# First mixture layer: twelve shared-expert chunks issued beside the first twelve expert tiles, and the ranks' results put in the logits' PSUM bank

## The chip, the cores and the metric

The kernel runs on one core of one Trainium2 chip. The metric is the time of one execution on the device in microseconds (us). The kernel before takes 1175.41 us, the median of three runs (1174.6 to 1175.93).

## The reference, cut to what matters

The program computes two transformer layers on x of 4 batches x 1024 tokens x 128 channels. The change touches only the feed-forward part of the first layer, a mixture of eight experts, two per token, with one shared expert that every token passes:

```python
logits = x_flat @ gate_w.T                      # 8 experts
scores = softmax(logits); in_topk = top 2       # w = scores * in_topk
gu = einsum('nh,eih->nei', x_flat, experts_gate_up); g, u = split(gu, 176)
out = einsum('nei,ehi->neh', silu(g) * u, experts_down) weighted by w
shared = silu(x_flat @ shared_gate_w.T) * (x_flat @ shared_up_w.T) @ shared_down_w.T   # width 352
out = out + sigmoid(x_flat @ shared_expert_gate_w.T) * shared
x = x + gb * out
```

## The kernel before, in words

The 4096 tokens are 32 tiles of 128 (NT = 32), 8 tiles to a batch (NB = 4 batches, TPB = 8). The mixture layer is one function, `layer_phase`, in which each engine has a queue written out by hand: first the engine's part of `route_parts`, then its part of `experts_parts`. Nothing but semaphores ties the queues together.

**Routing stage** (`route_parts`). For each batch b: VectorE computes statistics (L97 to L105) and the normalised rows h in two halves of four tiles (`rows`, L1297 to L1306); TensorE transposes each half into PSUM bank 0 (`transpose`, L1475), ScalarE copies it out to hT (L1411), TensorE makes the router's logits in bank 1 (`logits`, L1484); VectorE picks the top two (`experts_of`, L1312 to L1334); TensorE sums the ranks (`ranks`, L1490 to L1493) into bank 0, the transposes' bank; VectorE turns them into row numbers (`places`, L1340 to L1359), and GpSimd scatters the batch's rows to the buffer xg in memory by 16 indirect DMAs (L1232). Because `rank_ps` lies in bank 0, `transpose` of the next batch waits until the ranks of this one have been read (`ranked`).

**The shared expert** is cut into slabs of 512 tokens (8 of them) and its width of 352 into M = 3 chunks (128, 128, 96): 24 chunks n, `NU = 24`. A chunk is two products gate and up on TensorE (`up`, L1501, four matmul records of 512 columns), Silu on ScalarE (`shared`, L1430), the product on VectorE (`products`, L1368), and four matmuls of the down projection on TensorE (`down`, L1512, eight records). Three chunks accumulate one slab in bank 6 or 7 in turn; then ScalarE scales it out with four instructions (`shared_out`, L1438). The queues are: TensorE issues, for batch b, slab 2b, weights of expert 2b (`transpose_weights`, L1069 to L1076), transposes and logits of batch b+1, slab 2b+1, ranks of batch b+1, weights of expert 2b+1. So all 24 chunks are done before the first expert tile: the experts' TensorE part waits for `sh_out >= 8` at L1734 to L1742. The experts' weights and the chunks' gate/up results share banks 2 to 5 in turns; `pair_freed` says what a turn waits for.

**Tile stage** (`experts_parts`). 72 tiles of 128 gathered rows (NSLOT = 72). Tile n: SP loads 128 rows from xg (L1619); TensorE transposes them (`t_in`, L1734), ScalarE copies (L1641), VectorE copies the tile's expert weights (`lay_gate`, L1681), TensorE makes gate and up (`up`, L1742, six records), ScalarE Silu (L1652, L1653), VectorE the product (L1687 to L1690), TensorE down (L1759, four records), ScalarE scales (L1661), GpSimd scatters 128 rows to yk (L1632). The loops are skewed: TensorE's step n issues t_in(n+2), up(n+1), down(n-1). The first wave is tiles 0 to 39; their loads wait for the scatters of batches 0 to 2 and for VectorE's `tables`. GpSimd's queue holds all 64 row scatters ahead of the tiles' 72. VectorE also adds the finished shared expert to x, in eight instructions (L1698, L1703), one at each n = 8, 16, ... 64.

The second layer has the same two stages with other sizes; its work is as before.

Of the kernel before, what the change touches and what calls it, by code (L numbers as in the profile page):

```python
# [14 lines left out]
P = 128  # L15
# [975 lines left out]
NE = 8  # L991
# [13 lines left out]


# [98 lines left out]
def route_parts(nc, w, d, layer, ctx, bank):  # L1105
# [43 lines left out]
    rank_ps, total_ps = pT[:, 0:TPB * NE], pT[:, TPB * NE:TPB * NE + NE]  # L1149
# [11 lines left out]
    if layer == 0:  # L1161
# [5 lines left out]
        turn_of_chunk = lambda n: 2 + n + n // M  # L1167
        turn_of_weights = lambda e: 2 + (M + 1) * e + M
# [7 lines left out]
        def pair_freed(pe, turn, weights_out):  # L1176

            if turn < 2:
                return
            if turn < 4:  # L1180
                pe.wait_ge(weights_out, 1)
                return
            e, n = divmod(turn - 4, M + 1)
            if n == M:
                pe.wait_ge(weights_out, e + 2)
            else:
                pe.wait_ge(hid_done, M * e + n + 1)

        def weights_freed(pe, e, weights_out):
            pair_freed(pe, 0 if e == NE else turn_of_weights(e), weights_out)  # L1190
# [96 lines left out]

    def vector_part(dve):
# [73 lines left out]
        def products(s):  # L1362
            for n in range(M * s, M * s + M):
                cw = cols[n % M]
                dve.wait_ge(s_done, n + 1)

                after(dve, d_ps, n - 1)
                v.tensor_tensor(hid[n % 2][0:cw, :], sg[n % 2][0:cw, :], pg[0:cw, turn_of_chunk(n) % 2, 1, :], ALU.mult).then_inc(hid_done, 1)  # L1368

# [13 lines left out]
        for b in range(NB):  # L1383
            if layer == 0:
                for s in WEIGHTS_AT[b][0]:
                    products(s)
# [7 lines left out]
            if layer == 0:  # L1394
                for s in WEIGHTS_AT[b][1]:
                    products(s)
            if b + 1 < NB:
                places(b + 1)
                if b + 2 < NB:
                    rows(b + 2)  # L1400

    def scalar_part(act):
# [21 lines left out]
        def shared(s):  # L1424
            for n in range(M * s, M * s + M):
                cw = cols[n % M]
                act.wait_ge(g_ps, n + 1)

                after(act, hid_done, n - 1)
                nc.scalar.activation(sg[n % 2][0:cw, :], pg[0:cw, turn_of_chunk(n) % 2, 0, :], ACT.Silu).then_inc(s_done, 1)  # L1430
                if n % M == 1 and s > 0:
                    shared_out(s - 1)

        def shared_out(s):
            act.wait_ge(d_ps, M * (s + 1))
            for j in range(4):
                t = 4 * s + j
                ins = nc.scalar.activation(w.sh[:, t, :], pd[:, s % 2, j * C:(j + 1) * C], ACT.Copy, scale=w.shw[:, t:t + 1])  # L1438
            ins.then_inc(sh_out, 1)

# [12 lines left out]
        for b in range(NB):  # L1453
            for e in WEIGHTS_AT[b][0]:
                if layer == 0:
                    shared(e)
                copy_weights(act, e)
            if b + 1 < NB:
                batch(b + 1)
            for e in WEIGHTS_AT[b][1]:  # L1460
                if layer == 0:
                    shared(e)
                    if b + 1 < NB:
                        exponentials(b + 1)
                copy_weights(act, e)
        if layer == 0:
            shared_out(2 * NB - 1)

    def tensor_part(pe):
        def transpose(s):  # L1470
            pe.wait_ge(h_done, s + 1)
            after(pe, hT_done, s)
            after(pe, ranked, s // 2)
# [21 lines left out]

        def up(n):
            m, turn = n % M, turn_of_chunk(n)

            pair_freed(pe, turn, w_copied)
            for k in range(2):  # L1500
# [1210 lines left out]
```

## Time and profile before

| what | value |
|---|---|
| time of the runs, median of 3 | 1175.41 us (1174.6 to 1175.93) |
| span of the profiled execution | 1294.9 us |
| mean granted TensorE clock in it | 0.854 of full |
| ranks of batch 0 to first expert matmul, first layer (558.4 to 709.9) | 151.5 us |
| first expert matmul to the end of the tile stage (to 845.5) | 135.6 us |
| second layer's tile stage (1082 to 1262) | 180 us |

The profiled execution has no time of its own beside its span of 1294.9 us, so its own time is at least that; it is 119.5 us, 10.2%, above the median of the runs. In the profile, PE is the matmul side of TensorE, DVE is VectorE, ACT ScalarE, POOL GpSimd and SP the sync engine; ends of matmul records are modelled, and start times are what their spacing should be read from.

### The profile page before, as it was taken

To read this page: it belongs to the slowest core of one execution; us is meant where nothing else is said; L and a number is where in the kernel's file an instruction comes from. 1 tells how busy PE (TensorE), PEld (TensorE's weight loads), DVE (VectorE), ACT (ScalarE), POOL (GpSimd) and SP (SyncE) were. 2 spreads that over 40 slices of the span, in tenths; PEclk is the share of its full clock that TensorE was granted. 3 is DMA by queue.
4 is the path that set the end of the run, shared out by engine and by line. 5 is a ranking of instruction groups with operands and counts; after the bars stand their busy time and mean duration, and the time that the engine had idled before them with its cause. 6 is when DMAs were issued, how large, how long until landed. Compare 5 with 4: busy or idle time off the path is not lost. (4 is left out here: it accounts for less than half of the span.)

```text
span 1294.9 us, 26945 instructions
## 1 busy us (share of the span) xinstructions
PE 968.1 (75%) x9019; PEld 636.3 (49%) x9019; DVE 843.4 (65%) x2115; ACT 680.8 (53%) x1445; POOL 442.2 (34%) x510
## 2 busy tenths in 40 slices
PE   4656999999999999667576788718665427789990
PEld 2333333443343334344354677617543426679990
DVE  6897899999999996655431645556838555324444
ACT  3773678788788777324423555527022124436660
POOL 5626122332222122143234556510000733564440
PEclk9785799999999999867778989959687557989995
DMA  7235021111111000111110232276533311122216
GB/s 203 74 126 198 3 82 43 35 55 46 35 55 38 26 2 2 40 50 36 35 42 33 63 83 75 69 223 179 140 103 88 98 57 36 59 77 67 64 57 200
DMA packets 116285, 97.16 MB, mean 75 GB/s; under 512 B 15437, under 2 KB 102568, under 8 KB 116152
## 3 DMA queue, kind: packets, MB, share of 16 engines
q1 hardware_dynamic: 101912, 75.29, 20.4%
q0 software_dynamic: 8704, 17.97, 4.1%
q10 hardware_dynamic: 5536, 2.18, 0.6%
q8 instruction: 76, 1.25, 0.4%
q14 instruction: 57, 0.47, 0.1%
HBM read 60.18 MB, written 34.95 MB: 73 GB/s over the span
## 5 line engine op out<-in xcount | busy, mean ns | idle before, releaser
L568 DVE TENSOR_REDUCE part<-sps 128x2 f32<-128x1024 f32 (+2 forms) x307 | 327.6, 1115 | 27.0 <-PE sps L556 15.6
L911 ACT ACTIVATE prob<-tpa 128x1024 f32<-128x1024 f32 (+1 forms) x208 | 193.1, 928 | 45.1 <-PE tpa L857 43.3
L1632 POOL DMA_INDIRECT yk<-yo,place x144 | 146.6, 1018 | 158.1 <-ACT yo L1661 139.6
L743 POOL TENSOR_SCALAR_AFFINE_SELECT prob<-prob 128x512 f32<-128x512 f32 x128 | 80.5, 641 | 310.3 <-ACT prob L911 310.3
L1232 POOL DMA_INDIRECT xg<-h,slot x128 | 126.9, 991 | 152.1 <-DVE slot L1359 96.7
L877 PE MATMUL ops<-prob,vs 128*32 128x512 f32 (+3 forms) x1536 | 157.9, 498 | 0.1
L911 ACT ACTIVATE prob<-tpb 128x512 f32<-128x512 f32 (+1 forms) x224 | 127.2, 568 | 37.3 <-PE tpb L857 37.2
L549 PE MATMUL sps<-qk 48*128 48x512 bf16 (+2 forms) x734 | 132.9, 339 | 11.3 <-DVE part L568 7.6
L1687 DVE COPY place<-xt 128x1 uint32<-128x1 uint32 x144 | 22.1, 153 | 169.5 <-ACT esg L1655 92.5
L1748 PE MATMUL banks<-xT,y 128*128 128x128 f32 x864 | 113.8, 283 | 20.1 <-ACT y L1646 12.2
L1748 PEld LDWEIGHTS banks<-xT,y 128*128 128x128 f32 x864 | 106.5, 198 | 23.6 <-ACT xT L1641 19.3
L857 PE MATMUL tpa<-qk 50*128 50x512 bf16 (+3 forms) x512 | 85.6, 324 | 5.3 <-ACT prob L911 5.2
L857 PE MATMUL tpb<-qk 50*128 50x512 bf16 (+3 forms) x256 | 82.7, 343 | 5.2 <-DMA qk<-mrow 3.6
L1742 PE MATMUL banks<-xT,up_at 128*128 128x128 f32 (+1 forms) x432 | 68.3, 299 | 23.7 <-DVE up_at L1681 12.6
L1661 ACT ACTIVATE yo<-banks,xt 128x128 f32<-128x128 f32 x144 | 53.2, 369 | 45.8 <-PE banks L1759 35.8
L549 PEld LDWEIGHTS sps<-qk 48*128 48x128 bf16 x734 | 41.3, 94 | 71.9 <-DVE part L568 48.8
L1742 PEld LDWEIGHTS banks<-xT,up_at 128*128 128x128 f32 (+1 forms) x432 | 58.0, 202 | 31.2 <-ACT xT L1641 21.3
L556 PE MATMUL sps<-half 64*128 64x128 bf16 x976 | 66.5, 207 | 0.0
L857 PEld LDWEIGHTS tpa<-qk 50*128 50x128 bf16 x512 | 28.1, 94 | 69.3 <-ACT prob L911 61.2
L1759 PE MATMUL banks<-down,y 128*128 (+1 forms) x432 | 61.7, 281 | 0.2 <-issue 0.2
L556 PEld LDWEIGHTS sps<-half 64*128 64x128 bf16 x976 | 51.6, 97 | 20.8 <-issue 2.0
L1655 ACT ACTIVATE esg<-banks 128x384 f32<-128x384 f32 x72 | 35.5, 494 | 45.8 <-PE banks L1748 41.0
(347 smaller groups left out, 1864.8 us busy)
## 6 DMA issues: line engine op xcount, KB each, us to landing
xt<-xg SPq DMA_DIRECT2D x144, 65.0 KB
qk<-term SPq DMA_DIRECT2D x24, 256.0 KB, 2.6
qk<-qk SPq DMA_DIRECT2D x64, 96.0 KB
arena<-kpad SPq DMA_DIRECT2D x6, 1024.0 KB, 12.3
powers<-powr SPq DMA_DIRECT2D x8, 516.0 KB, 5.3
powr<-powers SPq DMA_DIRECT2D x4, 1032.0 KB, 9.3
qk<-qk SPq DMA_DIRECT2D x64, 64.0 KB
h<-yk SPq DMA_DIRECT2D x16, 256.0 KB, 4.9
```

The costliest lines, as they stand in the source:

```text
L549: ins = nc.tensor.matmul(out[:, s, at * wd:(at + 1) * wd], qk[lo:lo + KR, 0, x, i * P:(i + 1) * P], qk[lo:lo + KR, 1, x, c0:c0 + wd], star ...
L556: ins = nc.tensor.matmul(out[:, s, (at + 1) * wd - P + 64 * u:(at + 1) * wd], w.half[lo:lo + 64, 0, u, :], w.half[lo:lo + 64, 1, u, 64 * u ...
L568: return nc.vector.tensor_reduce(to, src, AX.X, ALU.max, negate=True)
L743: nc.gpsimd.affine_select(out=blk, in_=blk, pattern=[[0, HQ], [1, P]], compare_op=ALU.is_ge, fill=0.0, base=0, channel_multiplier=-1).then ...
L857: ins = nc.tensor.matmul(slot_of(t, m)[:, bank, col:col + n], qk[t % 4][lo:lo + KR + 2, 1, x, j * P:(j + 1) * P], qk[t % 4][lo:lo + KR + 2 ...
L877: ins = nc.tensor.matmul(ops[32 * h:32 * h + 32, o0:o0 + n], vs[t % 2][:, j, h, :], prob[:, PBUF[c] * HQ + u, col:col + n], start=c in OPE ...
L911: nc.scalar.activation(prob[:, at:at + len(units), 0:n], slot_of(t, m)[:, :, 0:n], ACT.Exp, scale=float(HD) ** -0.5).then_inc(exp_done, 1)
L1232: nc.gpsimd.indirect_dma_start(out=d.xg[layer], out_offset=bass.IndirectOffsetOnAxis(ap=w.slot[:, k, t:t + 1], axis=0), in_=w.h[k][:, t, : ...
L1632: nc.gpsimd.indirect_dma_start(out=d.yk, out_offset=bass.IndirectOffsetOnAxis(ap=place[:, u:u + 1], axis=0), in_=yo[u][:], in_offset=None) ...
L1742: ins = nc.tensor.matmul(pg[n % 2][0:cw, m * P:(m + 1) * P], up_at[n % WST][:, m * P:m * P + cw], xT[n % 4][:], start=True, stop=True)
L1748: ins = nc.tensor.matmul(out[:, m * P:(m + 1) * P], up_at[n % WST][:, (k * M + m) * P:(k * M + m + 1) * P], xT[n % 4][:], start=True, stop ...
L1759: ins = nc.tensor.matmul(pd[n % 2], hid[n % WST][0:cw, m, :], wt[0:cw, m, :], start=m == 0, stop=m == M - 1)
```

## The change

It has four parts. (1) In the first layer, only chunks 0 to 11 (slabs 0 to 3, `EARLY = 12`) stay in the routing stage, one slab per batch instead of two: chunk 3b ahead of batch b+1's transposes, chunks 3b+1 and 3b+2 and the last `down` behind its logits, the ranks behind them. Both weights of a batch go first. (2) Chunks 12 to 23 are issued in the tile stage, one in each of the steps n = 0 to 11, at the end of each engine's step (`late_tensor`, `late_scalar`, `late_vector`). They use one pair of banks (turn 1) and one accumulation bank, 6 (`bank_of_half`), so the first `down` of a late slab waits for the `shared_out` of the slab before it. (3) `rank_ps` and `total_ps` move to bank 1, with the logits; `transpose` no longer waits for `ranked`, and `logits` waits for it. The tile stage's transposes take one bank instead of two in the first layer, and t_in(n) waits for one copy more. (4) The eight additions of the shared expert to x come at n = 24, 28, ... 52 instead of n = 8, 16, ... 64.

```diff
+SUMS_AT = 24
-    WEIGHTS_AT = [([2 * b], [2 * b + 1]) for b in range(NB)]
+    WEIGHTS_AT = [([2 * b, 2 * b + 1], []) for b in range(NB)]
+    EARLY = M * NB
-    rank_ps, total_ps = pT[:, 0:TPB * NE], pT[:, TPB * NE:TPB * NE + NE]
+    rank_ps, total_ps = pl[:, P:P + TPB * NE], pl[:, P + TPB * NE:P + TPB * NE + NE]
+        bank_of_half = lambda s: s % 2 if s < NB else 0
+        TURNS = 2 + M
+        turn_of_weights = lambda e: TURNS * (e // 2) + e % 2
+        turn_of_chunk = lambda n: TURNS * (n // M) + 2 + n % M if n < EARLY else 1
...
 # VectorE, routing: products of chunk M*b ahead of tables/statistics/experts_of, the other two behind experts_of
+                shared_product(dve, M * b)
...
+                for n in range(M * b + 1, M * b + M):
+                    shared_product(dve, n)
...
 # ScalarE, routing
             for e in WEIGHTS_AT[b][0]:
                 copy_weights(act, e)
+                shared_silu(act, M * b)
             if b + 1 < NB:
                 batch(b + 1)
+                shared_silu(act, M * b + 1)
+                    exponentials(b + 1)
+                for n in range(M * b + 2, M * b + M):
+                    shared_silu(act, n)
+                shared_out(act, b)
...
+    def shared_down(pe, n):
+        m, s = n % M, n // M
+        pe.wait_ge(hid_done, n + 1)
+        if m == 0:
+            after(pe, sh_out, s if n >= EARLY else s - 1)
...
         def transpose(s):
-            after(pe, ranked, s // 2)
         def logits(s):
-            after(pe, lg_out, b)
+            after(pe, ranked, b)
...
 # TensorE, routing: both weights, shared_up(M*b), batch(b+1), then
+                for n in range(M * b + 1, M * b + M):
+                    shared_up(pe, n)
+                    shared_down(pe, n - 1)
+                shared_down(pe, M * b + M - 1)
+                if b + 1 < NB:
                     ranks(b + 1)
...
+    def late_tensor(pe, k):
+        if k <= NU - EARLY:
+            if k < NU - EARLY:
+                shared_up(pe, EARLY + k)
+            if k > 0:
+                shared_down(pe, EARLY + k - 1)
+    def late_scalar(act, k):
+        if k < NU - EARLY:
+            shared_silu(act, EARLY + k)
+        if k >= M + 1 and k % M == 1 and k <= NU - EARLY + 1:
+            shared_out(act, (EARLY + k) // M - 1)
+    def late_vector(dve, k):
+        if k < NU - EARLY:
+            shared_product(dve, EARLY + k)
...
 # experts_parts, first layer
-    pT, pd = [bank[:, 0, 0:P], bank[:, 6, 0:P]], ...
+    pT, pd = [bank[:, k, 0:P] for k in ((0, 0), (0, 6))[layer]], ...
-            after(pe, in_T, n - 1)
+            after(pe, in_T, n if layer == 0 else n - 1)
-                    pe.wait_ge(routed.sh_out, 2 * NB)
+                    pe.wait_ge(routed.hid_done, routed.early)
+                    pe.wait_ge(routed.sh_out, NB)
```

## Rows read from the trace of the kernel before

**Rows 1.** The page's first line

```profile
span 1294.9 us, 26945 instructions
```

**Rows 2.** Stretches of routing, then tile stage; columns PE, PEld, DVE, ACT, POOL, clock, DMA, GB/s

```profile
558.40:595.80 37.40, 27.50 (x95) 17.25 (x96) 16.34 (x77) 12.91 (x24) 16.31 (x16) 0.71 0.12 37
595.80:637.50 41.70, 26.40 (x111) 17.51 (x110) 16.82 (x77) 14.97 (x31) 15.37 (x16) 0.75 0.13 39
637.50:677.60 40.10, 26.99 (x113) 18.27 (x111) 18.38 (x80) 12.19 (x28) 15.64 (x16) 0.74 0.17 47
677.60:709.90 32.30, 20.64 (x102) 13.28 (x100) 7.28 (x20) 12.04 (x33) 15.37 (x16) 0.84 0.10 34
709.90:845.50 135.60, 107.89 (x790) 97.97 (x790) 70.56 (x315) 76.40 (x286) 75.46 (x71) 0.93 0.26 70
```

**Rows 3.** Waits of the routing stage: who for whom, us in total, times, longest

```profile
PE banks L1475 <- issue: 23.6, 3, 10.9
ACT sg L1430 <- remote: 9.0, 1, 9.0
```

**Rows 4.** Timelines of PE and ACT at batch 2's transposes: start, us, what, idle before

```profile
612.24 0.60 PE L1475 MATMUL banks<-ident,h 128*128 128x128 f32 x4
...
623.04 0.59 ACT L1411 COPY v<-banks 128x512 f32<-128x512 f32 x1 [6.28 <-remote]
```

**Rows 5.** Timelines of PE and POOL in the tile stage

```profile
714.82 0.83 PE L1742 MATMUL banks<-xT,up_at 128*128 128x128 f32 x6
...
716.04 0.83 PE L1742 MATMUL banks<-xT,up_at 128*128 128x128 f32 x6
...
845.35 0.96 POOL L1632 DMA_INDIRECT yk<-yo,place  x1 [0.30 <-issue]
```

**Rows 6.** The second layer's tile stage as one stretch

```profile
1082.00:1262.00 180.00, 161.89 (x1359) 158.60 (x1360) 67.78 (x237) 98.61 (x283) 90.77 (x93) 0.96 0.22 63
```

**Rows 7.** The stretch behind the late signal of rows 4

```profile
623.70:631.30 7.60, 7.58 (x24) 5.67 (x25) 3.03 (x31) 4.31 (x5) 0.00 (x0) 0.50 0.01 2
```

**Rows 8.** PE's timeline: two chunks that follow each other at full clock

```profile
632.27 1.88 PE L1501 MATMUL banks<-v,shgu 128*128 128x512 f32 x4
...
634.88 1.88 PE L1501 MATMUL banks<-v,shgu 128*96 128x512 f32 x4
```

**Rows 9.** DVE's timeline: the links of one batch's chain

```profile
549.74 0.69 DVE L1306 TENSOR_TENSOR h<-h,modr 128x512 f32<-128x512 f32 x1
...
552.75 0.17 DVE L105 SCALAR_TENSOR_TENSOR t<-t 128x8 f32<-128x8 f32 x1
...
554.86 0.23 DVE L1312 COPY lg<-banks 128x72 f32<-128x72 f32 x1 [1.94 <-PE banks L1484]
...
586.17 0.23 DVE L1312 COPY lg<-banks 128x72 f32<-128x72 f32 x1 [8.93 <-PE banks L1484]
...
589.68 0.19 DVE L1334 COPY run<-cum 128x8 bf16<-128x8 bf16 x1
...
598.29 0.22 DVE L1349 TENSOR_TENSOR row<-banks,first_row 128x64 f32<-128x64 f32 x1
...
604.77 1.28 DVE L1368 TENSOR_TENSOR hid<-sg,banks 128x512 f32<-128x512 f32 x2
```

**Rows 10.** ACT's timeline: table load, Silu of a chunk, a slab's four output instructions

```profile
679.82 1.28 ACT L1430 ACT_TABLE_LOAD   x1
681.11 0.60 ACT L1430 ACTIVATE sg<-banks 128x512 f32<-128x512 f32 x1
...
694.77 1.14 ACT L1438 ACTIVATE y<-banks,shw 128x128 f32<-128x128 f32 x4
```

**Rows 11.** Groups by line: the row scatters, and one half of the additions to x

```profile
L1232 POOL DMA_INDIRECT xg<-h,slot x64 | 62.7, 979 | 96.4 <-DVE slot L1359 78.1 <-issue 18.3
L1703 DVE TENSOR_TENSOR x<-x,y 128x1024 f32<-128x1024 f32 x4 | 4.8, 1211 | 0.0
```

**Rows 12.** POOL's timeline: the first of the row scatters

```profile
562.88 1.20 POOL L1232 DMA_INDIRECT xg<-h,slot  x1 [19.89 <-DVE slot L1359]
```

More of the change, by code:

```diff
@@ L1400, in vector_part, with shared_silu, shared_out @@
                     rows(b + 2)
+    def shared_silu(act, n):
+        cw = cols[n % M]
+        act.wait_ge(g_ps, n + 1)
+        after(act, hid_done, n - 1)
+        nc.scalar.activation(sg[n % 2][0:cw, :], pg[0:cw, turn_of_chunk(n) % 2, 0, :], ACT.Silu).then_inc(s_done, 1)
+    def shared_out(act, s):
+        act.wait_ge(d_ps, M * (s + 1))
+        for j in range(4):
+            t = 4 * s + j
+            ins = nc.scalar.activation(w.sh[:, t, :], pd[:, bank_of_half(s), j * C:(j + 1) * C], ACT.Copy, scale=w.shw[:, t:t + 1])
+        ins.then_inc(sh_out, 1)
     def scalar_part(act):
@@ L1422, in exponentials @@
             nc.scalar.activation(w.shw[:, s], lg[:, s, NE], ACT.Exp, scale=-1.0).then_inc(ex_done, 1)
[L1424 to L1439, printed above, removed]
         def batch(b):
@@ L1454, in scalar_part, with shared_up @@
             for e in WEIGHTS_AT[b][0]:
-                if layer == 0:
-                    shared(e)
                 copy_weights(act, e)
+            if layer == 0:
+                shared_silu(act, M * b)
             if b + 1 < NB:
                 batch(b + 1)
+            if layer == 0:
+                shared_silu(act, M * b + 1)
[4 more added lines that the diff above has]
+                shared_out(act, b)
             for e in WEIGHTS_AT[b][1]:
[L1461 to L1464, printed above, removed]
                 copy_weights(act, e)
-        if layer == 0:
-            shared_out(2 * NB - 1)
+    def shared_up(pe, n):
+        m, turn = n % M, turn_of_chunk(n)
+        if n < EARLY:
+            pair_freed(pe, turn, w_copied)
+        else:
+            pe.wait_ge(hid_done, n)
+        for k in range(2):
+            ins = nc.tensor.matmul(pg[0:cols[m], turn % 2, k, :], w.shgu[:, k, m * P:m * P + cols[m]], hT[:, n // M, :], start=True, stop=True)
+        ins.then_inc(g_ps, 1)
+    def shared_down(pe, n):
[3 more added lines that the diff above has]
+            after(pe, sh_out, s if n >= EARLY else s - 1)
+        for j in range(4):
+            ins = nc.tensor.matmul(pd[:, bank_of_half(s), j * C:(j + 1) * C], hid[n % 2][0:cols[m], j * P:(j + 1) * P],
+                                   w.shd[0:cols[m], m, :], start=m == 0 and j == 0, stop=m == M - 1, skip_group_check=True)
+        ins.then_inc(d_ps, 1)
     def tensor_part(pe):
@@ L1583, in experts_parts @@
     place = sb("place", [P, UN], U32)
[L1584 to L1585 removed]
+    pT, pd = [bank[:, k, 0:P] for k in ((0, 0), (0, 6))[layer]], [bank[:, 1, 0:C], bank[:, 7, 0:C]]
+    pg, pu = [bank[:, k] for k in ((2, 3), (2, 4))[layer]], [bank[:, 3], bank[:, 5]]
     x_in = [sem(f"xin{u}") for u in range(UN)]
@@ L1672, in scalar_part @@
                 y_copy(n - 1)
+            if layer == 0 and n >= 0:
+                routed.late_scalar(act, n)
     def vector_part(dve):
@@ L1776, in tensor_part @@
                 down(n - 1)
+            if layer == 0 and n >= 0:
+                routed.late_tensor(pe, n)
     made = Work()
```

78 lines of the change are left out of this document (25 added, 53 removed).

## The prediction

> **What bounds the kernel now.** First the span [rows 1] against the runs: 1294.9 us in the profiled execution, 1175.4 us in the median run. So 119.5 us of the profile are not in the metric, and a sum made from its rows has to say where they sit. Then the stretches [rows 2]: routing takes 151.5 us (558.4 to 709.9) and the 72 tiles 135.6 us. In no stretch of routing is any engine full: PE is busy 64 to 74%, at a granted clock of 0.71 to 0.84, which is a mix of the two levels 2.4 and 1.2 GHz; a chain across engines sets its pace, about 40 us a batch. Then who waits: GpSimd stands 78.1 us before its scatters for row numbers [rows 11], so the scatters follow the chain and do not lead it.
>
> Two waits do not look like work. PE stands 23.6 us in three waits before the second half of a batch's transposes, with nothing shown as releaser, and ACT 9.0 us once before a Silu ("remote") [rows 3]. One of them: the matmuls of the transposes are recorded to 612.84, and the copy that waits for their signal starts at 623.04 [rows 4]. The tile stage has the same in small: two tiles can start 1.22 us apart, and an indirect DMA takes 0.96 us and 0.30 us to the next, 1.27 us [rows 5], so 72 tiles need 91.4 us and take 135.6. In the second layer a tile has 19 matmul records (12 gate and up, 6 down, 1 transpose) at 0.11 us (six of them fill 0.66 of the 1.22 us in rows 5), 2.1 us, or 151 us for 72, and takes 180 [rows 6]. These excesses, 44 + 29 + 32.6, make 106 of the 119.5 us. I therefore take them for a cost of being profiled, and work the change out without them; that they are real is the first rival. By the Trainium skill, "Runtime: NRT & Kernel Launch", The ~15µs preamble/postamble breakdown, a profile's total stands about 6.2 us over the reported time whatever the kernel is; here it is 119.5 us, so the trace disagrees, and by the rule the stalls would be in the runs too.
>
> **The routing stage before, as the runs see it.** 151.5 - 32.6 = 118.9 us. Behind each late signal PE goes on at half clock: 7.6 us at 0.50 after it had been idle for 10.9 us [rows 7, 3], which costs 3.8 us, less behind the shorter ones; three times about 3 us. That leaves **110 us**.
>
> **The routing stage after.** Per batch the chain is:
> - from the end of the rows h (550.43) to the copy of the logits (554.86) 4.4 us at half clock; about 3.3 at full, where VectorE's product (1.28 for two) and statistics (550.4 to 552.9) fill it [rows 9];
> - `experts_of` 3.7 us (586.17 to 589.87) [rows 9], hidden behind PE from here on;
> - from the logits to the ranks: up, down, up, down, down, with Silu and product between. A chunk is 2.61 us of PE at full clock [rows 8], about 1.73 up and 0.88 down. At half clock up, down, up are 8.7 us, then Silu 0.6, product 0.7, down 1.8, ranks 0.2: 12.0. At full clock ScalarE leads instead: up 1.7, then three table loads of 1.28, two Silu of 0.6 [rows 10] and two exponentials, taken at 0.25 each (the least instruction of rows 10 is 1.14 / 4), then product, down and ranks 1.8: 9.0;
> - places and the next rows h, 6.6 us (598.3 to 604.8, where the next products begin) [rows 9].
>
> Sum 23.0 us at half clock, 18.9 at full. The clock before was 0.71 to 0.75 in these stretches [rows 2], half the time at either level; I take 21, three times, and 1 for the tables: 64. I see no reason for a lower or a higher clock, but this is the least certain term. After the ranks of batch 3: two experts' weights, ten transposes, 1.4 (an estimate from 0.11 to 0.14 us a record), three chunks 7.9, the last Silu, product and down 2.2, the outputs 1.14 and signals: 13. Routing after **77 us** (70 to 83). The scatters go on at 0.98 + 0.30 us each [rows 11]; 48 of them from the first at 562.9 [rows 12] end at 624, and with a load of some 2 us tile 0 could start at 627, just before 558.4 + 77 = 635: not the bound. So the change takes 110 - 77 = **33 us** out of the routing stage (27 to 41: the first with the half-clock chain, the second without the subtraction for rows 7).
>
> The bank of the ranks: the transposes lose their wait for `ranked`, the logits get it. `ranked` comes with L1349, 6 us before the next rows end [rows 9], so both waits are long satisfied: 0. The wait that t_in gains (one copy more) stands in front of an `up` that waits for the same copy: 0, at most the 0.11 us of one transpose a tile, 8 us in all if every tile stood there. The weights' turns and the second batch of weight transposes ahead of the chain sit in VectorE's `places` and rows: 0.
>
> **The tile stage after.**
> - The twelve chunks: PE has 2.61 us more a tile where it had 1.22 us of work in 1.27. It is then the bound, GpSimd and the others have room (ScalarE gets 0.6 and a third of 1.14, VectorE 0.7): 12 x 2.61 - 12 x 0.05 = **+30.7 us**.
> - A new wait: with one accumulation bank the first `down` of slabs 5, 6 and 7 waits until ScalarE has put out the slab before. ScalarE does that behind the Silu of the chunk whose `up` PE has just issued, so PE stands for a Silu 0.60, four outputs 1.14 [rows 10] and about 0.3 of signals: 2.04 us, three times, **+6.1 us**. Behind PE in that time: the next tile's transpose and matmuls, and with them all engines.
> - The clock behind these waits and at the start of the stage: **+2 us** (0 if it stays full; a chunk and a tile at half clock cost 3.8 us more, three times 11).
> - The additions to x are as many, 1.21 us each [rows 11], but four tiles apart. VectorE has (70.6 - 8 x 1.21) / 72 = 0.85 of 1.27 us to do in a tile [rows 2], so four tiles give back 1.7 us: 0, at most 4 us if a tile is tighter than that.
> - Nothing changes in SP's queue. On GpSimd's, the 16 scatters of batch 3 now run beside the first tiles, whose own scatters are queued behind them; eight output buffers cover some 30 us at 3.9 us a tile: 0.
>
> **Sum.** -33 + 30.7 + 6.1 + 2 = +5.8 us. The work itself is only moved, PE has as much of it as before; the change gains where PE stood idle in routing and gives back as much in a stage where PE has no idle time. From 1175.4 us: **1181.2 us**. In the profile's own terms the stages would shorten and lengthen by other amounts, as the late signals come on top.
>
> **Rivals.**
> 1. *The tile stage has slack in the runs too* (the other side). If the 135.6 us of the tile stage are real, a tile is 1.88 us and a chunk adds 1.22 + 2.61 - 1.88 = 1.95 us: 12 x 1.95 = 23.4, with 6.1 of waits and no clock cost, against 33: -3.5 us, 1172; with 37 saved in routing 1168. For: the rows show that gap, and some 0.6 us of each tile. Against: the 119.5 us must be somewhere, and these gaps with their like in routing and the second layer make 106 of them. It decides once a tile takes over 1.7 us in the runs.
> 2. *Half clock through routing and the first tiles.* Routing has half its matmuls taken out and PE stands idle in between. Chain 23 us, so 27 saved instead of 33, and 11 instead of 2 in the tile stage: +20.8, 1196 with everything, 1189 with half of it. For: after 10.9 us of idling the clock was 0.50 [rows 7]. Against: a tile stage granted 0.93. The Trainium skill, "TensorE: Matmul & The Clock Gate", HAM oscillation, says that work cut into pieces with idling between them starts each piece at half rate, and advises to keep TensorE fed; rows 7 agree for a long idle time, and by that rule routing would take the 23 us chain throughout.
> 3. *It cancels.* The waits for `shared_out` are short or the routing chain is at full clock: 33 to 41 saved against 37 to 39: within 2 us, 1175.
> 4. *The scatters gate the first tile.* If each took a fifth more, 48 would end at 636 and tile 0 start at 639, 4 us behind the ranks' chain: 1185, inside the forecast. It counts in the forecast and caps what a faster chain could gain.
>
> **How the numbers follow.** Forecast (small loss, 1178 to 1188) 0.42; rival 2 0.15; rival 1 0.26; rival 3 0.17. Differences under 0.2%, 2.35 us, are what a measurement of this kernel can't tell from none. Rival 1 lies mostly below 1173, rival 3 within the bound for the greater part; the forecast's and rival 2's cases are slower except at their lower edge. Faster 0.28, same 0.17, slower 0.55. The range takes rival 1 down to 1168 and rival 2 up to 1191.
>
> **What would show it.** In the changed kernel's profile: ranks some 21 to 25 us apart where they stood 37 to 42 apart, first expert matmul 30 to 60 us earlier (the late signals go in part as well); twelve steps of 3.9 us or more; PE waiting about 2 us for ScalarE's L1438 outputs ahead of the first `down` of slabs 5, 6, 7; the remaining 60 tiles as before. I would be wrong if the tile stage grew by clearly less than 30 us, if the routing chain turned out to be held by something other than these links, or if those three waits were absent.

## The result and the profile after

| | before | changed |
|---|---|---|
| median of 20 runs each, us | 1174.19 (1170.12 to 1179.66) | 1177.71 (1174.13 to 1181.92) |

The ratio is 1.003, 95% interval 1.0018 to 1.0042: 2.1 to 4.9 us slower, where 1181.2 (1168 to 1191) was forecast. The page's first line for the changed kernel:

```profile
span 1173.3 us, 26944 instructions
```

That execution took 1174.6 us, 1.3 us over its span, and lies among its kernel's other runs. The 1294.9 us of [rows 1] are explained by the first experiment: the kernel before was run and profiled again, unchanged. It gave this first line:

```profile
span 1176.4 us, 26945 instructions
```

In this study the kernel before takes either 1174 to 1178 us or 1294 to 1297 us, in whole series of runs (below); in each series the profiled execution lies among the other runs of its kernel. The trace ahead of the prediction comes from the second condition, the result from the first. I call them the **quick** and the **slow condition**, and compare each kernel with runs of before from its own series. All stage times are read from single profiles: routing is the first ranks to the first expert matmul, the tile stage runs from there to the last down projection.

The stretches of the kernel before in the quick condition (columns as in rows 2: length, busy PE, PEld, DVE, ACT, POOL, granted clock, DMA, GB/s): routing, tiles 0 to 11, 12 to 23, 24 to 39, 40 to 71:

```profile
563.20:668.90 105.70, 87.78 (x413) 56.40 (x413) 58.84 (x251) 51.83 (x113) 59.59 (x61) 0.91 0.18 54
668.90:689.00 20.10, 15.74 (x125) 14.10 (x126) 13.74 (x66) 11.60 (x44) 11.48 (x13) 1.00 0.24 68
689.00:705.40 16.40, 15.53 (x134) 14.68 (x132) 10.87 (x50) 13.11 (x50) 12.24 (x13) 1.00 0.36 96
705.40:733.20 27.80, 23.51 (x176) 21.59 (x176) 15.32 (x68) 17.77 (x65) 17.87 (x17) 0.94 0.38 99
733.20:779.90 46.70, 43.07 (x357) 40.42 (x358) 30.14 (x134) 34.98 (x129) 35.66 (x33) 1.00 0.32 87
```

The same five stretches of the changed kernel, same condition:

```profile
559.20:632.60 73.40, 59.78 (x269) 39.48 (x269) 50.73 (x239) 40.67 (x84) 53.11 (x53) 0.83 0.22 65
632.60:681.00 48.40, 42.77 (x250) 30.70 (x250) 21.40 (x80) 23.05 (x69) 20.46 (x22) 1.00 0.20 53
681.00:700.90 19.90, 19.14 (x154) 17.25 (x153) 9.81 (x45) 14.29 (x52) 10.17 (x11) 1.00 0.24 68
700.90:730.70 29.80, 23.61 (x178) 21.71 (x178) 17.37 (x68) 17.57 (x65) 19.54 (x17) 0.94 0.34 89
730.70:777.00 46.30, 42.33 (x359) 40.26 (x358) 30.43 (x134) 35.19 (x130) 35.10 (x33) 1.00 0.32 89
```

Line by line: routing -32.3 us; the first 24 tiles 68.3 against 36.5, +31.8; the rest +2.0 and -0.4. PE's busy time tells why the gain comes back: it falls by 28.0 us in routing and rises by 27.0 in the first twelve tiles and 3.6 in the next twelve. The work was moved from one stage in which PE had 17.9 us of idle time to one in which it had 4.4. And routing still leaves PE idle for 13.6 of its 73.4 us: of the 32.3 us gained there, 28.0 are work that went elsewhere and only 4.3 are idle time.

The changed kernel's timeline of PE: the ranks of batches 0 to 3, the first tile's transpose and gate/up, the chunk `up` ahead of the first wait, the first `down` of slabs 5, 6 and 7, and between them the gate/up of two tiles that follow each other, each with a chunk:

```profile
559.16 0.24 PE L1514 MATMUL banks<-run,trib 128*128 128x64 bf16 x1 [1.66 <-DVE cum L1342]
...
581.95 0.20 PE L1514 MATMUL banks<-run,trib 128*128 128x64 bf16 x1
...
601.39 0.20 PE L1514 MATMUL banks<-run,trib 128*128 128x64 bf16 x1
...
619.81 0.20 PE L1514 MATMUL banks<-run,trib 128*128 128x64 bf16 x1
...
631.45 0.30 PE L1758 MATMUL banks<-ident,xt 128*128 128x128 f32 x1 [0.70 <-DMA xt<-xg]
...
632.58 0.90 PE L1766 MATMUL banks<-xT,up_at 128*128 128x128 f32 x6
...
649.12 1.88 PE L1479 MATMUL banks<-v,shgu 128*128 128x512 f32 x4
...
652.81 1.13 PE L1490 MATMUL banks<-shd,hid 128*128 128x128 f32 x8 [1.81 <-ACT y L1417]
...
657.72 0.83 PE L1766 MATMUL banks<-xT,up_at 128*128 128x128 f32 x6
...
661.55 0.83 PE L1766 MATMUL banks<-xT,up_at 128*128 128x128 f32 x6
...
666.36 1.13 PE L1490 MATMUL banks<-shd,hid 128*128 128x128 f32 x8 [1.81 <-ACT y L1417]
...
679.90 1.13 PE L1490 MATMUL banks<-shd,hid 128*128 128x128 f32 x8 [1.81 <-ACT y L1417]
```

The ranks stand 22.8, 19.4 and 18.4 us apart. A tile with a chunk takes 3.83 us, which is 1.22 of its own work and the 2.61 of the chunk. The three waits for the one accumulation bank are there, at the places named, 1.81 us each. ACT's timeline of the first of them shows what they are made of: the Silu of the chunk just issued, and only behind it the four outputs that free the bank:

```profile
651.04 0.60 ACT L1411 ACTIVATE sg<-banks 128x512 f32<-128x512 f32 x1 [1.21 <-PE banks L1479]
651.53 1.14 ACT L1417 ACTIVATE y<-banks,shw 128x128 f32<-128x128 f32 x4
```

The two whole times do not differ as the medians do (1173.3 against 1176.4, where the medians go up by 3.5). The first ranks come at 559.2 in the one and at 563.2 in the other, before any changed instruction but the order of the weights; in the other profiles of this study they come at 557.8 to 561.1, whichever kernel it is. From the first ranks on, the changed kernel's profile is 0.9 us longer.

### The profile page after: what moved, and what is told of

Its sections match the earlier page's. It is cut to its first block and busy times, and to the rows that moved or that the text cites. A ratio compares the mean times of both kernels' runs of the same rounds, so it can differ in the third digit from the quotient of the medians.

```text
span 1173.3 us, 26944 instructions
## 1 busy us (share of the span) xinstructions
PE 936.6 (80%) x9019; PEld 614.2 (52%) x9019; DVE 844.3 (72%) x2115; ACT 685.2 (58%) x1445; POOL 441.4 (38%) x510
## 5 line engine op out<-in xcount | busy, mean ns | idle before, releaser
L1652 POOL DMA_INDIRECT yk<-yo,place x144 | 146.6, 1018 | 112.6 <-ACT yo L1681 91.3
L549 PE MATMUL sps<-qk 48*128 48x512 bf16 (+2 forms) x734 | 132.4, 338 | 12.8 <-DVE part L568 7.4
L1772 PE MATMUL banks<-xT,y 128*128 128x128 f32 x864 | 110.4, 278 | 1.5 <-DVE y L1703 1.2
L1766 PE MATMUL banks<-xT,up_at 128*128 128x128 f32 (+1 forms) x432 | 61.6, 279 | 4.3 <-ACT xT L1661 3.3
L1766 PEld LDWEIGHTS banks<-xT,up_at 128*128 128x128 f32 (+1 forms) x432 | 53.5, 189 | 6.6 <-ACT xT L1661 4.2
```

What stands on the lines that cost most here:

```text
L549: ins = nc.tensor.matmul(out[:, s, at * wd:(at + 1) * wd], qk[lo:lo + KR, 0, x, i * P:(i + 1) * P], qk[lo:lo + KR, 1, x, c0:c0 + wd], star ...
L1652: nc.gpsimd.indirect_dma_start(out=d.yk, out_offset=bass.IndirectOffsetOnAxis(ap=place[:, u:u + 1], axis=0), in_=yo[u][:], in_offset=None) ...
L1766: ins = nc.tensor.matmul(pg[n % 2][0:cw, m * P:(m + 1) * P], up_at[n % WST][:, m * P:m * P + cw], xT[n % 4][:], start=True, stop=True)
L1772: ins = nc.tensor.matmul(out[:, m * P:(m + 1) * P], up_at[n % WST][:, (k * M + m) * P:(k * M + m + 1) * P], xT[n % 4][:], start=True, stop ...
```

## The experiments

They were made in four series; the medians of before in them were 1177.61 (17 runs), 1296.95 (26), 1294.25 (17) and 1176.67 (19). "After" in a diff is the changed kernel.

**Before, unchanged, profiled again** (no edit).

> The kernel before, unchanged, profiled once more. My theory (the late signals of the first profile are a cost of that profiled execution, not of the runs): span about 1173 us instead of 1294.9; from the first ranks to the first expert matmul 106 to 112 us instead of 151.5, its ranks 28 to 31 us apart; tile stage 91 to 97 us instead of 135.6. Rival 1 (the stalls are real and the tile stage has slack): tile stage 120 us or more again, PE idle before transposes in routing.

1177.71 us, one run, span 1176.4. Routing takes 105.7 us and the tile stage 111.0, not 151.5 and 135.1 as in the trace of [rows 2], and no wait for an absent releaser like that of [rows 3] is left in routing: PE's waits before the transposes are 2.9 us in all. So the late signals do not come with a profile as such. The tile stage missed what I expected: 111.0 us and not 91 to 97.

**Outputs ahead of the Silu** (after, with the two blocks of `late_scalar` exchanged):

```diff
     def late_scalar(act, k):
+        if k >= M + 1 and k % M == 1 and k <= NU - EARLY + 1:
+            shared_out(act, (EARLY + k) // M - 1)
         if k < NU - EARLY:
             shared_silu(act, EARLY + k)
-        if k >= M + 1 and k % M == 1 and k <= NU - EARLY + 1:
-            shared_out(act, (EARLY + k) // M - 1)
```

> The changed kernel with one order turned round: in the late steps ScalarE puts out a finished slab ahead of the next chunk's Silu, not behind it. My theory (the three waits of 1.81 us before the first down of slabs 5, 6, 7 are a real cost on the path, and only the order makes them): the three waits shrink to under 0.3 us each, the twelve chunk steps take 49 us instead of 54.3, the time is 1172.3 us, 5 us under the changed kernel and 1 to 2 us under the kernel before. Rival (PE's time there is hidden by something else, the wait moves to ScalarE or GpSimd): 1177 us, no change.

1172.61 us (12 runs), ratio to before 0.9964 (0.9944 to 0.9984), where the changed kernel's is 1.003: some 5 to 8 us less (the first by the medians of two series, the second by the ratios). Its stretch of the first twelve tiles:

```profile
635.70:678.60 42.90, 42.71 (x250) 30.74 (x250) 20.93 (x79) 22.91 (x69) 19.14 (x20) 1.00 0.20 54
```

48.4 us become 42.9, with PE idle for 0.2. The three waits were all but 0.2 us of PE's idle time there, and without them the change gains: the sign of its effect in this condition hangs on them.

**Without the late chunks** (after; the three calls of `late_scalar`, `late_vector`, `late_tensor` removed, so that slabs 4 to 7 of the shared expert are left out):

```diff
-                routed.late_scalar(act, n)
...
-                routed.late_vector(dve, n)
...
-                routed.late_tensor(pe, n)
...
-                    dve.wait_ge(routed.sh_out, 2 * NB)
+                    dve.wait_ge(routed.sh_out, NB)
```

> The changed kernel with chunks 12 to 23 left out altogether (slabs 4 to 7 of the shared expert are not computed and the sums add stale data there). My theory: the late chunks cost 12 x 2.61 + 3 x 1.8 = 36.8 us, so about 1141 us; the difference to the kernel before, 33 us, is then what the routing stage gained, first expert matmul about 73 us after the first ranks as in the changed kernel, tile stage 92 to 95 us. Rival 1 (slack in the tile stage): the chunks cost 24 to 29 us, so 1149 to 1153 us.

1148.74 us (4 runs), ratio 0.9767 (0.9732 to 0.9802). Routing and the first twelve tiles:

```profile
559.00:635.20 76.20, 60.70 (x269) 40.53 (x269) 51.94 (x239) 40.67 (x84) 54.92 (x56) 0.83 0.23 67
635.20:655.70 20.50, 16.78 (x125) 15.62 (x125) 13.01 (x65) 11.81 (x45) 15.62 (x17) 0.92 0.35 89
```

The routing side alone is worth 28.9 us in the runs, and the tiles behind it take what they took before (20.5 against 20.1). The chunks therefore cost some 31 us in the runs (1.003 less 0.9767, of 1177), 32.3 in the profiles (144.4 against 112.1). Gain and price are separate and nearly equal. I had expected 36.8 us for the chunks and a time of 1141; it came out beside the rival's 1149, so the tile stage has some slack, though not the rival's cost of 24 to 29 us.

**The late chunks as one block ahead of the tiles** (after; the calls moved from the loops to loops of their own in front of them):

```diff
+        if layer == 0:
+            for k in range(routed.early + 1):
+                routed.late_tensor(pe, k)
         for n in ...:
...
-                routed.late_tensor(pe, n)
```

The calls of ScalarE and VectorE are moved likewise.

> The changed kernel with the twelve late chunks issued in one block between the routing stage and the first tile instead of one in each tile step. My theory (PE is the bound in both and the tile stage hides next to nothing of a chunk): the block takes about 12 x 2.65 us plus three waits for outputs and the drain of its chain, less the 1 to 2 us that PE waits for the first tile's load; 1178 to 1184 us, within 0.5% of the changed kernel. Rival 1 (riding beside tiles hides 0.6 us or more of each chunk): 1186 us or more.

1190.72 us (4 runs), ratio 1.014 (1.0098 to 1.0183). The block, and its two longest sets of waits:

```profile
632.00:677.80 45.80, 33.25 (x143) 19.35 (x143) 8.87 (x14) 11.56 (x29) 11.14 (x12) 1.00 0.10 27
```

```profile
DVE hid L1298 <- ACT sg L1411: 37.3, 12, 4.0
ACT sg L1411 <- PE banks L1479: 31.6, 11, 3.0
```

I had taken a block to cost what riding costs. It costs 45.8 us with PE busy for 33.25: with one pair of banks, the gate and up of a chunk wait until Silu and product of the chunk before have read it, so ACT, DVE and PE take turns. Of PE's 12.6 idle us, 5.2 are `up` waiting for the product of the chunk before, and 5.4 the three waits for the outputs, which riding has as well. Riding, the tiles' matmuls fill these turns and the same chunks cost 31.8. So with one pair of banks the interleaving makes the chunks cheap; a block with more banks was not tried.

**Additions to x eight tiles apart, from tile 14** (after):

```diff
-SUMS_AT = 24
+SUMS_AT = 14
-            if layer == 0 and SUMS_AT <= n < SUMS_AT + 4 * 2 * NB and n % 4 == 0:
+            if layer == 0 and SUMS_AT <= n < SUMS_AT + 8 * 2 * NB and n % 8 == SUMS_AT % 8:
```

> The changed kernel with the eight additions to x eight tiles apart again (n = 14, 22, ... 70) instead of four. Theory (a tile has room on VectorE for 1.21 us in four tiles, so the spacing costs little): the stretch from expert tile 24 to 40, 29.8 us in the changed kernel against 27.8 in the clean profile of before, falls by 1 us, and the time by 0 to 2 us, 1176 to 1178. Rival (each addition stands on the path, its 1 us comes at any spacing): no change at all in the tile stage.

This series found the slow condition. 1286.94 us (8 runs), ratio 0.9937 (0.9906 to 0.9968) with before at 1296.95, the median of 26 runs. The 1294.9 us of [rows 1] are thus the time of a condition that the runs have too. Tiles 24 to 39:

```profile
746.40:778.10 31.70, 23.48 (x176) 21.50 (x177) 14.86 (x65) 16.81 (x64) 17.28 (x17) 0.95 0.31 81
```

The changed kernel takes 36.6 us for these tiles in the slow condition, but the whole tile stage is 172.1 us here and 173.0 there, and the ratios are 0.9937 and 0.9938. In the quick condition the same spacing, in the last experiment, takes 29.7 against 29.8 us for these tiles. So no gain from the spacing is seen in either. What an addition costs can be read in the changed kernel's timelines, quick condition, of VectorE and PE:

```profile
721.80 1.21 DVE L1720 TENSOR_TENSOR y<-y,gate 128x1024 f32<-128x1024 f32 x1
...
722.93 0.34 DVE L1703 COPY up_at<-up 128x368 f32 x1
...
723.37 0.90 PE L1766 MATMUL banks<-xT,up_at 128*128 128x128 f32 x6 [0.65 <-ACT xT L1661]
```

The copy of the next tile's weights stands behind the addition in VectorE's queue, and PE waits for it: from one tile's gate/up to the next it is 2.28 us here and 1.22 to 1.29 beside it. (The view names ScalarE's copy as what ended the wait; VectorE's ended last, at 723.27.) In the kernel before, with eight tiles between additions, such tiles take 2.28 us too, and 1.9 to 2.3 in the last experiment. This is the rival of this run's expectation, that the 1 us of an addition comes at any spacing: both kernels pay for eight, so it all but cancels.

**Outputs first, and the ranks ahead of the last two `down`** (the edit above, and in TensorE's routing queue):

```diff
-                for n in range(M * b + 1, M * b + M):
-                    shared_up(pe, n)
-                    shared_down(pe, n - 1)
-                shared_down(pe, M * b + M - 1)
+                shared_up(pe, M * b + 1)
+                shared_down(pe, M * b)
+                shared_up(pe, M * b + 2)
                 if b + 1 < NB:
                     ranks(b + 1)
+                shared_down(pe, M * b + 1)
+                shared_down(pe, M * b + 2)
```

> The kernel of the second experiment (outputs ahead of the Silu), and TensorE issues the ranks of a batch ahead of the last two downs of its slab. Theory (the routing stage of the changed kernel is held at its end by the row scatters of batches 0 to 2, 48 at 1.28 us and a load, not by TensorE's chain): ranks come 17 to 18 us apart instead of 18.4 to 22.8, but the first expert matmul comes at most 2 us earlier, and the time is that of the second experiment within 2 us. Rival (the chain of ranks sets the end of routing): first expert matmul 5 us earlier, time 5 us under the second experiment.

1284.1 us (7 runs), ratio 0.9915 (0.9886 to 0.9945); routing 112.6 us, tile stage 162.1. The changed kernel has 106.6 and 173.0 in this condition (below), and the run before this one, with the same routing, 105.4 and 172.1. So the tile stage is shorter, but routing, which the edit was to shorten, is 6 to 7 us longer. The ratio can't be told from the changed kernel's 0.9938 (0.9914 to 0.9962). The edit was repeated in the quick condition, last in this section.

**Before, with one bank for the tiles' transposes:**

```diff
-    pT, pd = [bank[:, 0, 0:P], bank[:, 6, 0:P]], ...
+    pT, pd = [bank[:, k, 0:P] for k in ((0, 0), (0, 6))[layer]], ...
-            after(pe, in_T, n - 1)
+            after(pe, in_T, n if layer == 0 else n - 1)
```

> The kernel before with one part alone: the first layer's tile transposes in one bank instead of two, each waiting for one copy more. Theory (the transpose stands in front of an up that waits for the same copy, so the wait costs nothing): tile stage 111 us as in the clean profile of before, time within 2 us of before. Rival (it couples PE and ScalarE tighter, and part of the longer tiles of the changed kernel is this): tile stage 2 to 8 us longer.

1295.15 us (10 runs), ratio 0.9976 (0.995 to 1.0001). The tile stage, against 135.6 in [rows 2] (135.1 to the same point, the start of the last `down`):

```profile
711.00:843.70 132.70, 104.85 (x791) 95.08 (x790) 70.54 (x315) 76.68 (x286) 74.69 (x70) 0.97 0.27 72
```

In this condition the bank costs nothing, as the sum had it (0, at most 8). This series was slow, where the tiles have slack; in the quick condition, in which the metric was taken, the bank was not tried alone.

**Before, with the ranks in the logits' bank:**

```diff
-    rank_ps, total_ps = pT[:, 0:TPB * NE], ...
+    rank_ps, total_ps = pl[:, P:P + TPB * NE], ...
-            after(pe, ranked, s // 2)        # transpose
-            after(pe, lg_out, b)             # logits
+            after(pe, ranked, b)
```

> The kernel before with the other part alone: ranks in the logits' bank, the transposes without their wait for the ranks being read, the logits with it. Theory (both waits are long satisfied): ranks 28 to 29 us apart as in the clean profile, time within 2 us of before. Rival (the transposes stood behind that wait): ranks 1 us closer, 3 us in all.

1297.57 us (10 runs), ratio 1.0015 (0.999 to 1.004). Its routing stage as one stretch:

```profile
559.60:713.60 154.00, 99.38 (x413) 64.73 (x413) 59.08 (x251) 52.02 (x113) 62.28 (x64) 0.78 0.13 39
```

154 against 151.5 us, and 153.2 in the run before with its routing unchanged: it gains nothing and costs nothing that can be told. With the one before, in this condition, the effect is left to the place of the chunks and of the weights.

**The changed kernel again** (no edit), the third series, again in the slow condition.

> The changed kernel, unchanged, once more. The experiments so far showed two kinds of chip: on one the kernel before takes 1174 to 1178 us, on another 1297 us, with the late TensorE signals of the first profile in the runs too. Theory (the late signals leave slack in the tile stage, which is my first rival's case): where before takes about 1297 us, the changed kernel is 6 to 12 us faster (ratio 0.991 to 0.995); where before takes about 1175 us, it is 1 to 5 us slower (1.001 to 1.004). Rival (the changed kernel's effect does not depend on the chip): the same ratio near 1.003 on either.

1287.44 us (6 runs) against 1294.25, ratio 0.9938 (0.9914 to 0.9962): **here the change is faster**, by 6.8 us. Routing, tiles 0 to 11, and tiles 24 to 39:

```profile
561.00:667.60 106.60, 70.35 (x268) 48.07 (x269) 50.80 (x239) 40.66 (x84) 58.39 (x60) 0.72 0.17 53
667.60:723.30 55.70, 46.59 (x250) 33.08 (x250) 21.26 (x80) 22.90 (x69) 13.47 (x14) 0.94 0.11 31
745.50:782.10 36.60, 26.86 (x177) 24.93 (x178) 17.50 (x68) 17.78 (x66) 20.08 (x17) 0.86 0.27 73
```

Routing falls from 151.5 to 106.6, 44.9 us, and the tile stage grows from 135.1 to 173.0, 37.9; together -7.0. What the slow condition adds to each stage is the difference to the quick one: in routing 45.8 us before and 33.2 after, in the tile stage 24.0 and 28.6. The change shortens the stage in which signals are late, and so loses 12.6 us of lateness there for 4.6 more among the tiles: -8.0, to which the work itself adds the +1.1 of the quick condition (the sum is the -7.0 within rounding). These are single profiles; that it is faster rests on the runs.

**Three edits together, slow condition** (outputs first, ranks ahead of the last two `down`, additions eight tiles apart).

> The changed kernel with three edits: outputs ahead of the Silu, ranks ahead of the last two downs, additions eight tiles apart. Theory: at a chip of the fast kind 1170 to 1172 us (5.4 from the waits, 1 from the spacing, little from the ranks, since the scatters hold the end of routing), ratio 0.993 to 0.997; at a chip of the slow kind 12 to 18 us under before, ratio 0.986 to 0.991. Rival (the ranks' order helps in full): 3 to 5 us better than that.

1285.69 us (12 runs), ratio 0.9933 (0.9903 to 0.9964): 8.6 us under before, less than I wrote. Routing took 119.9 us in its profile and the tile stage 156.3, against 106.6 and 173.0 of the changed kernel. Both profiles with the ranks ahead of the last two `down` have a longer routing in this condition (112.6 and 119.9) than both without (106.6 and 105.4); why was not found. It is part of why the three edits gain no more here than the changed kernel does.

**Before, with plain stores of the tiles' results** in place of the scatters to yk (same bytes; the rows land elsewhere, so the second half of the layer reads other values):

```diff
-        nc.gpsimd.indirect_dma_start(out=d.yk, out_offset=..., in_=yo[u][:], in_offset=None).then_inc(y_out[u], 16)
+        pool.dma_start(d.yk[n * P:(n + 1) * P, :], yo[u][:]).then_inc(y_out[u], 16)
```

> The kernel before with the tiles' 144 indirect scatters (both layers) replaced by plain transfers of the same 64 KB each from the same queue, to consecutive rows, so that results land at other places than the combination reads. It asks what the late TensorE signals of the slow kind of chip hang on. Theory (they come with indirect scatters in flight, since routing and tile stages show them and the attention stage, as dense on TensorE, does not): on the slow kind both tile stages lose them and shorten by 25 to 40 us each; on the fast kind the first tile stage goes from 111 us to 95 to 105 us, because the 1.27 us of a scatter no longer bind. Rival (they hang on dense 32-bit matmuls whatever the transfers are): on the slow kind the tile stage stays above 125 us with signals over 1 us late.

It was meant for the slow condition, and its series found the quick one. 1170.79 us (10 runs), ratio 0.9952 (0.9932 to 0.9972). Its tile stage:

```profile
664.00:775.00 111.00, 96.35 (x790) 89.30 (x790) 70.23 (x316) 77.35 (x285) 42.32 (x75) 1.00 0.33 88
```

POOL's busy time falls to 42.3 us and the stage takes 111.0, as before, not the 95 to 105 I had expected. The 1.27 us from scatter to scatter of [rows 5] is not what sets a tile's pace. The 6 us in the median are not in this stage; in the two profiles 3.2 lie ahead of the first ranks and 1.7 in routing, where nothing edited has run yet, and 1.3 behind the second layer's tiles. So what the edit itself is worth stays open. On the late signals of the slow condition, for which it was made, this run says nothing.

**Three edits together, quick condition.**

> The three edits once more, for the other kind of chip if this one is it: where before takes about 1175 us, 1170 to 1172 us, ratio 0.994 to 0.998, and routing no shorter than the second experiment's 74.7 us by more than 2 us, as the scatters of batches 0 to 2 hold its end; where before takes about 1295 us, 0.990 to 0.996 as in the run before.

1170.49 us (8 runs), ratio 0.9938 (0.9918 to 0.9958). Routing and the whole tile stage:

```profile
559.70:632.40 72.70, 56.88 (x268) 38.07 (x269) 50.68 (x239) 40.72 (x84) 52.36 (x53) 0.88 0.22 66
632.40:771.50 139.10, 128.08 (x934) 110.87 (x934) 78.12 (x327) 90.14 (x314) 83.38 (x81) 0.98 0.29 77
```

The tile stage is 5.3 us shorter than the changed kernel's, as with the outputs first alone. The ranks of batch 3 come 6.2 us sooner (613.6 against 619.8), and the first expert matmul only 0.2 us sooner. The timelines of PE and of POOL show why:

```profile
626.48 1.16 PE L1490 MATMUL banks<-shd,hid 96*128 96x128 f32 x8 [0.51 <-DVE hid L1298]
...
631.39 0.30 PE L1759 MATMUL banks<-ident,xt 128*128 128x128 f32 x1 [3.75 <-DMA xt<-xg]
```

```profile
625.24 0.96 POOL L1237 DMA_INDIRECT xg<-h,slot  x1 [0.30 <-issue]
```

PE is done with the chunks at 627.6 and waits 3.75 us for the first tile's rows, whose load waits for the 48th scatter, issued at 625.2. That is rival 4: it caps what a shorter chain of ranks can give. This version beats both kernels in the quick condition; its interval overlaps that of the outputs first alone (0.9944 to 0.9984), so what the other two edits add is not shown. In the slow condition it lies beside the changed kernel.

## Why the prediction came out as it did

The direction was right, the size 2.3 us too large (+5.8 for +3.5). Term by term, in the quick condition, in which the metric was taken:

| step of the prediction | predicted, us | measured, us |
|---|---|---|
| routing before, without the late signals | 110 | 105.7 |
| routing after | 77 (70 to 83) | 73.4 |
| out of routing | -33 | -32.3 |
| twelve chunks | +30.7 | +26.4 |
| three waits for the outputs | +6.1 | +5.4 |
| clock in the tile stage | +2 | 0 |
| additions, banks, scatters, the remaining tiles | 0 | +1.6 |
| sum | +5.8 | +1.1 by the two profiles' stages, +3.5 (2.1 to 4.9) by the runs |

One profile's routing is good to 2 or 3 us: with the same instructions in it, it takes 73.4, 74.7 and 76.2 us in the changed kernel and the second and third experiments, and 105.7 and 104.0 in before and before with plain stores. With these the sum is +1.1 to +5.6, so it does not contradict the runs.

- **"I therefore take them for a cost of being profiled"**: this step was wrong in its reason. A profile of the same kernel in the quick condition has none of the late signals, and in the slow condition the medians of runs are 1294 to 1297 us, as the profile was. They are real there; the 1175.4 us of the metric and the trace beside it came from different conditions. Taking them out was right for the number and only by that accident. That the excesses of 44, 29 and 32.6 us summed to nearly the 119.5 was luck too: between the two profiles of before the first tile stage differs by 24.0, the second by 25.1, routing by 45.8, and the second layer's routing, which the sum left out, by 28.3. The sign of the change hangs on it: 1.003 in the one condition, 0.9938 in the other.
- **Routing before and after**: the two figures, one by subtraction and one by links, were 4.3 and 3.6 us too high, and the errors cancel. The batches stand 28.6, 28.8 and 27.6 us apart before and 22.8, 19.4 and 18.4 after, 60.6 in all for 63 in the sum; the end from the ranks of batch 3 on takes 12.8 for 13. Half the time at either level would be a granted clock of 0.75; the three batches had 0.79 on average, and it rises batch by batch: 0.68, 0.82, 0.91 and 1.00 in the four parts of routing. Two slips in the readings moved nothing: PE's least share of routing in [rows 2] is 63% and not 64, and the upper end of the saving, 110 + 9 - 77, is 42 and not 41.
- **The chunk term was mis-sized**: "where it had 1.22 us of work in 1.27". A tile takes 1.54 us on average in the quick condition (111.0 / 72). In the first 24 tiles before, PE is idle for 4.4 + 0.9 = 5.3 us, and the chunks fill that: 12 x 2.61 = 31.3 less 5.3 is 26.0, with 5.4 of waits 31.4, for 31.8 measured. I had left 0.6 of slack where there were 5.3. The plain stores show that the scatters do not set the pace; yet most tiles do take 1.22 to 1.29 us, and the chunk steps 3.83. The slack sits in a few tiles, where VectorE has more to do than a tile's own work. In the kernel before, quick condition, these are tiles 6 to 9 (VectorE makes the second wave's `tables` there) and 10 and 18 (additions), with 1.84 to 2.42 us each:

```profile
678.20 0.17 DVE L1254 TENSOR_TENSOR nt<-nt,done 128x8 f32<-128x8 f32 x1
...
678.66 0.35 DVE L1681 COPY up_at<-up 128x368 f32 x1 [0.29 <-DVE nt L1254]
...
679.11 0.90 PE L1742 MATMUL banks<-xT,up_at 128*128 128x128 f32 x6 [1.04 <-ACT xT L1641]
```

PE stands 1.04 us for the weights that VectorE copies behind the tables, up to 679.01 (again the view names ScalarE's copy, done at 678.67). Under a chunk's 2.61 us of PE work such work of VectorE is hidden; that is why the chunks cost 26.4 us and not 30.7.

- **The waits**: 1.81 for 2.04 us, at the place and for the reason given, and removed by exchanging two blocks.
- **The clock**: granted 1.00 in both stretches with chunks. The 1.81 us waits and the change of stage did not lower it, so the 2 us were not there. That full clock is also what decides rival 2. The Trainium skill, "TensorE: Matmul & The Clock Gate", HAM oscillation, warns that work cut into pieces with long waits between them starts each at half rate. Routing after is work in pieces too, though PE's longest wait in it is 1.8 us; it starts at 0.68, but by its end the clock is full, and the forecast's half-and-half chain was nearer than half clock throughout.
- **Rival 1** named the slow condition's numbers (a tile of 1.88 us) and a gain of 3.5 to 7.5. There the gain is 6.8, but not by its mechanism: the first twelve tiles grow by 33.8 us, not by 23.4 + 6.1, as late signals come with the chunks too; it is routing that gives 44.9 and not 33 to 37.
- **Rival 3**, it cancels, holds for the work itself (+1.1 in the profiles); the runs put the difference at 0.3% (0.18 to 0.42), and it is the three waits that carry it there.
- **Rival 4** is no price in the changed kernel (PE waits 0.70 us for the first load) and the limit of the next improvement.
- **Zero terms**: both banks are confirmed alone, in the slow condition only. The additions' term came out near zero, but not because four tiles give back 1.7 us: each addition costs its tile about 1 us, in both kernels. Four of them lie in tiles 24 to 39 of the changed kernel and two in the same tiles of before, which would make the +2.0 us there; but the last experiment, also with two, takes 29.7 us, with PE standing 3.2 us once for a load. So where the +2.0 come from stays open.

## What to carry to other kernels

Moving work from a stage that a chain bounds to one in which the same engine is nearly full gives back what it gains: compare the idle time of that engine in both, before anything else (17.9 us and 4.4 here, for 31 us of work), and afterwards see how much of the first has gone (4.3 us). What was left to win lay, for the greater part, in the order of two blocks in one queue: what frees a bank goes ahead of what only feeds the next step. And where a profile's span and the median of the runs differ by 10%, first run the old kernel again beside its profile: which of the two describes the chip decides the sign of a small change.

## What the runs showed of the hardware

**Two conditions.** The same kernel takes 1174 to 1178 us in some series and 1294 to 1297 us in others, and no series changed from one to the other. What lies ahead of routing, with the first layer's attention, takes the same in both (first ranks at 557.8 to 563.2 us). The difference of 118.5 us between the two profiles of before lies in routing (45.8), the tile stage (24.0) and what follows it (53.5), less 4.8 ahead of routing. Of the 53.5, the second layer's routing has 28.3 (79.4 against 51.1) and its tile stage 25.1 (180.8 against 155.7), while the 158 us between the two layers' mixtures, with the second attention, are the same within 0.2. In the slow condition an engine can go on several us after the records end of the matmuls that it waits for (10.2 us in [rows 4]). Three rows of the changed kernel's waits in routing, slow condition (us in total, times, longest), and ACT's timeline of one:

```profile
ACT sg L1411 <- remote: 23.2, 3, 11.3
...
ACT y L1417 <- remote: 13.5, 2, 6.9
...
DVE lg L1325 <- remote: 12.0, 2, 8.0
```

```profile
612.81 0.60 ACT L1411 ACTIVATE sg<-banks 128x512 f32<-128x512 f32 x1 [11.32 <-remote]
```

The releaser "remote" on a kernel of one core marks such waits in these traces; the longest, of ACT in the three edits' slow profile, is 26.9 us. All four stages that grow have GpSimd's indirect DMAs in flight, and the stretches without them do not grow; that these DMAs are the cause was not shown, since the run that replaced the tiles' scatters fell into the quick condition. The record numbers the chip of each series: 12, 6, 12 and 12. Number 12 was quick, then slow, then quick again within an hour, so if it is one chip each time, the condition is no fixed property of it; what sets it stays open.

**The clock follows.** Before's routing stage is granted 0.91 in the quick condition and 0.71 to 0.84 in its parts in the slow one [rows 2]: it is lower behind the idle time of a late signal (0.50 in [rows 7]). For the same matmuls PE is busy 101.5 us there and 87.8 in the quick condition, so some 14 of the 45.8 us are a lower clock and the rest waiting.
